# A graph network's last three edge passes: TensorE's gather of a batch cut into parts between its other products

## The chip, the cores and the metric

One core of a Trainium2 chip runs the kernel. TensorE multiplies matrices, VectorE (DVE) and ScalarE (ACT) do elementwise work, GpSimd (POOL) issues indirect DMAs, SyncE (SP) issues the other DMAs. The metric is the device time in microseconds of one launch, of which the median of three runs is given.

## The reference

Four graph networks run one after the other on 6250 nodes with 16 features and 206,250 edges sorted by target node, each followed by a residual sum and a layer norm. The kernel numbers its edge passes 0 to 9: pass 0 is the first network, passes 1 to 6 the second, pass 7 the third, passes 8 and 9 the two rounds of the fourth. The last two networks are those that the change touches:

```
# third: pass 7
msg = inputs[src] * timestamp
h = jax.ops.segment_max(msg, dst, num_segments=inputs.shape[0])
x = layernorm(x + h @ W.T + b)

# fourth: its first layer is computed in pass 7, the rounds are passes 8 and 9
w = relu(edgefeats @ fnet_w1 + fnet_b1) @ fnet_w2 + fnet_b2
W = w.reshape(-1, 16, 16)
for _ in range(2):
    xj = hx[edge_src]
    m = einsum('ei,eio->eo', xj, W)
    agg = segment_sum(m, edge_dst, num_segments=n_nodes) * inv_deg
    hx = gru_cell(agg, hx, ...)
```

## The kernel before

**Batches.** The edges lie in tiles of 128. A batch has `HT` = 8 tiles, 1024 edges, and there are `NB` = 202 batches in each of passes 7, 8 and 9. The engines run their own instruction streams, in the order in which the code issues them, and wait on semaphores. The order is written out by hand; for these three passes there is no planner. Each engine does one loop body a batch: `maxima(k)` in pass 7, `messages8(k)` (ScalarE: `next_hot(k)`) in passes 8 and 9.

**Where the source features come from.** Each tile needs the 16 features of its 128 source nodes. Five of the eight tiles of a batch (`FETCHED`) get them by an indirect DMA of GpSimd (L781). The other three (`GT`, 384 edges) get them from TensorE, in four steps. VectorE makes one-hot rows of the source's block with seven `tensor_scalar` operations (`hot_rows`, L1635; two buffers `hot8`). TensorE multiplies them with the node table `x8`, which is cut into three bf16 pieces: 6 blocks x 3 pieces = 18 products of 384 columns (L835) and a last one with 96 rows (L836), all added up in one PSUM bank, `picked_rows` (`gather8`). VectorE keeps of each sum the row of the right node (`select8`, L1644) and writes it to SBUF (`picked_by`, two buffers). TensorE turns the result with three fp32 products, which the profile shows as six (`turn8`, L845), and ScalarE copies it from PSUM (`copy8`, L1464).

**The order and its waits.** There is one bank `picked_rows`. `gather8(p, j)` waits until the one-hot rows of batch j are made (`hot8_made`) and until batch j - 1 was selected (`selected`), and signals `picked` with its last product. `select8(p, j)` waits for `picked` of j, `turn8(p, j)` for `selected` of j and the copy of j - 1. All this runs ahead of the batch that uses it: in the body of batch k, TensorE turns batch k + 3 (`AHEAD` = 3) and gathers batch k + 4; VectorE makes the one-hot rows of k + 5 and selects k + 4. The first four gathers come before the loop (`open_gather`).

**TensorE's other work in a batch.** Segment products (`segments`, L824): eight fp32 products, shown as 16, which add the values of batch k - 1 into two open PSUM banks by target node. They wait for the masked values of VectorE (`split_blocks`, L1538) and the one-hot of ScalarE (`one_hot`, L1435). In pass 7: a transpose into the scan (L1122), one out of it (L1138), and the first layer of the fourth network, four row-tiled products (L1130, shown as eight), after which ScalarE applies the relu (L1485) and stores the result. In passes 8 and 9: the messages, bias products (L1170) and second-layer products (L1174), into four banks, in two halves, each with a signal; VectorE multiplies them with the source features in four operations (L2197) and adds up (L2204).

TensorE's order in a batch before the change is, in pass 7: transpose in, turn of k + 3, first layer, gather of k + 4, segment products of k - 1, transpose out. In passes 8 and 9: messages of k, turn of k + 3, gather of k + 4, segment products of k - 1.

VectorE's order is, in pass 7: values of k - 1, two steps of the reset, weighted message of k + 1, scan (L2164), carry, one-hot rows of k + 5, select of k + 4. In passes 8 and 9: four multiplications, one-hot rows of k + 5, reduction, select of k + 4, values of k. ScalarE's is, in pass 7: copy of k + 3, relu of the first layer, eight squares (L1429), store, one-hot; in passes 8 and 9: squares, copy of k + 3, one-hot.

Of the kernel before, what the change touches and what calls it, by code (L numbers as in the profile page):

```python
# [47 lines left out]
NB = -(-TE // (2 * HT)) * 2  # L48
# [16 lines left out]
GC = GT * P  # L65
FETCHED = HT - GT
AHEAD = 3
STRIPS = 4
SE = HE // STRIPS
BL = 7  # L70
BLANES = P
LAST = BL - 1
# [35 lines left out]
def build(nc, a, out):  # L108
# [12 lines left out]
    with ctx:  # L121
# [688 lines left out]
        def _(pe):  # L810
# [5 lines left out]
            def segments(p, k, h):  # L816

                pe.load(out_at, base[0:1, ds(k * HT + HT, HT)])
                outs = [pe.snap(r, min_val=0, max_val=2 * CH - 32) for r in out_at]
                pe.wait_ge(scl[p].sem, scl[p].at(k - 1, APER[p]))  # L820
                pe.wait_ge(vec[p].sem, vec[p].at(k + 1, VALUES7) if p == 7 else vec[p].at(k, VALUES8))
                pe.sem_inc(pe_go, 1)
                for u in range(HT):
                    last = mm(sums[:, ds(outs[u], 32)], hot[h][:, u, :], masked[h][:, u, :, :].rearrange("p b f -> p (b f)"),  # L824
                              start=False, stop=False)
                last.then_inc(ten[p].sem, 1)

            def gather8(p, j):

                pe.wait_ge(hot8_made[p], j + 1)  # L830
                pe.wait_ge(selected[p], j)
                pe.sem_inc(pe_go, 1)
                for b in range(LAST):
                    for i in range(3):
                        mm(picked_rows, x8[:, b, i, :], hot8[j % 2][:, b, :], start=b == i == 0, stop=False)  # L835
                last = mm(picked_rows, x8[0:STACKED, LAST, 0, :], hot8[j % 2][0:STACKED, LAST, :],  # L836
                          start=False, stop=True)
                last.then_inc(picked[p], 1)

            def turn8(p, j):  # L840

                pe.wait_ge(selected[p], j + 1)
                pe.wait_ge(copied[p], j)
                for u in range(GT):
                    last = mm(turned_rows[:, u * 16:(u + 1) * 16], picked_by[j % 2][:, u * P:(u + 1) * P], pick_f,  # L845
                              start=True, stop=True)
                last.then_inc(turned[p], 1)
# [263 lines left out]
            p = 7  # L1111
# [5 lines left out]
            def maxima(k):  # L1117
                h = k % 2

                pe.wait_ge(vec[p].sem, vec[p].at(k - 1, VPER[p] if k == 0 else MSG))  # L1120
                pe.wait_ge(vec[p].sem, vec[p].at(k - 1, SCAN))
                nc.tensor.transpose(ps[:, 4, 0:P], msg[h][:, :, :].rearrange("p u f -> p (u f)"), w["ident"][:, :]  # L1122
                                    ).then_inc(ten[p].sem, 1)
                if k + AHEAD < NB:
                    turn8(p, k + AHEAD)
                pe.wait_ge(loaded[h], load_count(p, k))
                pe.wait_ge(scl[p].sem, scl[p].at(k - 1, RELU7))
                pe.sem_inc(pe_go, 1)
                for i in range(STRIPS):
                    last = mm(ps[32 * i:32 * i + 32, 7, 0:SE], w["f1"][32 * i:32 * i + 13, :], edges[h][32 * i:32 * i + 13, :],  # L1130
                              start=True, stop=True)
                last.then_inc(ten[p].sem, 1)
                if k + AHEAD + 1 < NB:
                    gather8(p, k + AHEAD + 1)
                segments(p, k - 1, 1 - h)
                pe.wait_ge(vec[p].sem, vec[p].at(k, SCAN))
                pe.sem_inc(pe_go, 1)
                nc.tensor.transpose(ps[:, 6, 0:P], wk[:, HE:HE + P], w["ident"][:, :]).then_inc(ten[p].sem, 1)  # L1138
# [16 lines left out]
            for p in (8, 9):  # L1155
                pe.wait_ge(ready, SETUP + 3 + 2 * (p - 7))
                pe.wait_ge(bias_cut, BIAS_CUT)
                stage_done(pe, PHASES[p])
                open_sums()
                ten[p].open(pe)  # L1160
                open_gather(p)
                def messages8(k):
                    h = k % 2

                    pe.wait_ge(loaded[h], load_count(p, k))
                    for strips, used in ((range(2), MUL[1]), (range(2, STRIPS), MUL[3])):
                        pe.wait_ge(vec[p].sem, vec[p].at(k - 1, used))
                        pe.sem_inc(pe_go, 1)
                        for i in strips:
                            mm(ps[:, 4 + i, :], ones16[32 * i:32 * i + 32, :],  # L1170
                               bias3[32 * i:32 * i + 32, :].unsqueeze(1).to_broadcast([32, 2, 256]), start=True, stop=False)
                        for v in range(2):
                            for i in strips:
                                last = mm(ps[:, 4 + i, v * 256:(v + 1) * 256], strip[h][32 * i:32 * i + 32, v * P:(v + 1) * P],  # L1174
                                          w["w2b"][32 * i:32 * i + 32, :], start=False, stop=v == 1)
                        last.then_inc(ten[p].sem, 1)

                    if k + AHEAD < NB:
                        turn8(p, k + AHEAD)
                    if k + AHEAD + 1 < NB:  # L1180
                        gather8(p, k + AHEAD + 1)
                    segments(p, k - 1, 1 - h)

                for k in range(NB):
                    messages8(k)
                segments(p, NB - 1, 1)
                close_sums()
                turn_sums(p)
                name = PHASES[p + 1]
                for c in range(2):  # L1190
                    pe.wait_ge(*after(name, c, 2))
                    for g in range(2):
                        mm(bank(c, g), ih_pk[g], t_pk[:, pcs(c)], start=True, stop=False)
                        mm(bank(c, g), hh_pk[g], hidden(p)[:, pcs(c)], start=False, stop=True)
                    mm(bank(c, 3), ih_pk[2], t_pk[:, pcs(c)], start=True, stop=True)
                    mm(bank(c, 2), hh_pk[2], hidden(p)[:, pcs(c)], start=True, stop=True).then_inc(packed[name][c], 1)
                if p == 8:
                    packed_rows(name, 10, h_pk)
                else:
                    packed_norm(name, 11)  # L1200
                    packed_rows(name, 18, x_pk)
# [3 lines left out]
        def _(act):  # L1205
# [273 lines left out]
            cut8(7)  # L1479
            def maxima(k):  # L1480
                h = k % 2
                if k + AHEAD < NB:
                    copy8(7, k + AHEAD)
                act.wait_ge(ten[7].sem, ten[7].at(k, F7))
                act_fn(rst, ps[:, 7, 0:SE], ACT.Relu, bias=w["fb1"][:, :]).then_inc(scl[7].sem, 1)  # L1485
                squares(7, k + 1, 1 - h, rel_last)
                act.wait_ge(scl[7].sem, scl[7].at(k, RELU7))
                act.dma_start(rT[:, ds(k * SE, SE)], rst).then_inc(r_out, 16)
                act.wait_ge(ten[7].sem, ten[7].at(k, SEG7))
                one_hot(7, k + 1, 1 - h)  # L1490
                act.wait_ge(r_out, k * 16 + 16)

            for k in range(NB):
# [6 lines left out]
            for p in (8, 9):  # L1500
                open_one_hots(p, rel)
                cut8(p)
                def next_hot(k):
                    h = k % 2
                    squares(p, k + 1, 1 - h, rel)
                    if k + AHEAD < NB:
                        copy8(p, k + AHEAD)
                    act.wait_ge(ten[p].sem, ten[p].at(k, SEG8))
                    one_hot(p, k + 1, 1 - h)

                for k in range(NB):
                    next_hot(k)
                join(p)
                name = PHASES[p + 1]
                for c in range(2):
                    act.wait_ge(*after(name, c, 3))
                    for g in range(2):
                        act_fn(gates[:, g, pcs(c)], bank(c, g), ACT.Sigmoid, bias=bias_pk[:, 4 + g:5 + g])
                    act_fn(gates[:, 2, pcs(c)], bank(c, 2), ACT.Identity, bias=bias_pk[:, 3:4]).then_inc(packed[name][c], 1)
                packed_one(name, 6, u_pk, t_pk, ACT.Tanh, bias=bias_pk[:, 2:3])  # L1520
                if p == 8:
                    packed_rows(name, 11, 3)
                else:
                    packed_norm(name, 11)
                    packed_rows(name, 19, 4)
# [765 lines left out]
```

## Time and profile before

| what | value |
|---|---|
| median of 3 runs | 8719.59 us (8715.59 to 8722.13) |
| profiled execution, first to last instruction | 10879.2 us |
| time of that execution apart from its span | not given |
| TensorE's mean granted clock | 0.867 of full speed |
| pass 7, scans from / to | 5140.4 / 6915.0 us |
| pass 8, reductions from / to | 7072.1 / 8879.9 us |
| pass 9, reductions from / to | 9036.9 / 10829.0 us |

The profile is of one execution, whose span is longer than the time of the runs without a profiler. Its times are in microseconds from its first instruction unless marked ns. PE is TensorE, PEld its weight loads. In a timeline each row is a group of like instructions: start, duration, engine, line, operation, what it writes and reads, and behind [ the idle time of the engine before it and what ended that. "issue" is a wait that nothing in the profile explains, "remote" one that was ended by a semaphore update whose maker the profile doesn't tell. In a row of windows stand the stretch, its length, the busy time of PE, PEld, DVE, ACT and POOL with the number of instructions, the granted clock of TensorE as a share of full speed, the DMA engines' busy share and GB/s. The ends of products are modelled.

### The profile page before, as it was taken

How to read it: one execution, taken by the hardware profiler on the slowest of the kernel's cores; microseconds unless marked ns; L12 is line 12 of the kernel's file. 1: busy time of each engine (PE TensorE's matmuls, PEld its weight loads, DVE VectorE, ACT ScalarE, POOL GpSimd, SP SyncE). 2: the span in 40 equal slices, each digit the busy share in tenths (PEclk: the TensorE clock that was granted, in tenths of full speed). 3: DMA queues.
4: the chain of work that ended last, by engine and by line, in shares of the span. 5: the costliest groups of instructions: out<-in, count | busy, mean ns of one | idle time of the engine just before them, and what ended most of it. 6: DMA issues, size and time to landing. Idle time of an engine off the chain costs nothing.

```text
span 10879.2 us, 202778 instructions
## 1 busy us (share of the span) xinstructions
PE 8956.7 (82%) x67778; PEld 6273.6 (58%) x67782; DVE 6315.3 (58%) x13443; ACT 3593.0 (33%) x10701; POOL 4698.0 (43%) x4703
## 2 busy tenths in 40 slices
PE   1588877888887999974888888599999977999998
PEld 0345544555555878862565556466666655666666
DVE  2577766777763222222444444377777766777877
ACT  5233322333330011000444444344443433444444
POOL 1456555666560000003555555355555535555552
PEclk9889988999996999975888888788888888888888
DMA  9522233222228978994222222111111111111111
GB/s 315 165 77 80 80 87 83 82 82 81 79 71 327 323 277 282 321 354 155 63 62 63 62 62 63 41 42 41 41 42 41 42 34 35 42 42 42 42 41 33
DMA packets 915020, 1169.57 MB, mean 108 GB/s; under 512 B 245746, under 2 KB 807652, under 8 KB 913804
## 3 DMA queue, kind: packets, MB, share of 16 engines
q1 hardware_dynamic: 720778, 1086.22, 30.9%
q0 software_dynamic: 150336, 28.94, 3.4%
q10 hardware_dynamic: 43202, 44.90, 1.3%
q8 instruction: 456, 7.47, 0.3%
q14 instruction: 248, 2.03, 0.1%
HBM read 1025.39 MB, written 133.22 MB: 106 GB/s over the span
## 4 chain that ended last, share of the span: by engine, by line
PE 50%; issue 6%; DVE 6%; another core or an unknown queue 5%; DMA 3%; ACT 1%; SPq 0%; DVEq 0%; ACTq 0%
PE ps L835 18%; PE ps L1036 9%; PE ps L824 8%; PE ps L845 4%; PE ps L1174 4%; DMA arena<-adj 3%; PE ps L1053 1%; PE ps L1170 1%; PE ps L1130 1%; DVE msg L2204 1%; PE ps L1047 1%; PE ps L836 1%; DVE dinv L1635 1%; DVE invdeg L1635 1%
## 5 line engine op out<-in xcount | busy, mean ns | idle before, releaser
L781 POOL DMA_INDIRECT arena<-tab,x_all x3030 | 2951.3, 974 | 4504.7 <-DMA tab<-stage 2048.9
L799 POOL DMA_INDIRECT adj<-acc x1616 | 1693.0, 1048 | 1266.4 <-DVE acc L1851 721.7
L835 PE MATMUL ps<-invdeg,acc 128*128 128x384 bf16 x5454 | 1202.4, 387 | 154.9 <-issue 154.5
L835 PE MATMUL ps<-dinv,acc 128*128 128x384 bf16 x5454 | 1221.2, 392 | 95.8 <-issue 49.2
L1246 ACT ACTIVATE wide<-ps,not_all 128x128 bf16<-128x128 f32 x1616 | 658.2, 419 | 1552.1 <-remote 1030.9
L1644 DVE SCALAR_TENSOR_TENSOR dinv<-x_all,ps 128x384 f32<-128x384 f16 x606 | 368.3, 608 | 1160.5 <-remote 825.0
L835 PEld LDWEIGHTS ps<-invdeg,acc 128*128 128x128 bf16 x5454 | 619.0, 118 | 697.2 <-issue 485.6
L835 PEld LDWEIGHTS ps<-dinv,acc 128*128 128x128 bf16 x5454 | 624.2, 119 | 651.6 <-issue 449.1
L1429 ACT ACTIVATE arena<-w_iota,rel 128x128 f32<-128x128 f32 x3232 | 988.2, 388 | 13.1
L845 PE MATMUL ps<-x_all,dinv 128*128 128x16 f32 x3636 | 585.9, 287 | 398.8 <-issue 290.8
L845 PEld LDWEIGHTS ps<-x_all,dinv 128*128 128x128 f32 x3636 | 537.7, 220 | 579.2 <-issue 450.6
L913 PE MATMUL ps<-arena 128*128 128x128 f32 x3232 | 481.9, 294 | 360.3 <-issue 180.5
L1435 ACT ACTIVATE acc<-arena,unit 128x1024 f32<-128x1024 f32 x303 | 348.0, 1149 | 1190.0 <-PE ps L824 433.1
L1435 ACT ACTIVATE arena<-arena,unit 128x1024 f32<-128x1024 f32 x303 | 348.1, 1149 | 1183.4 <-PE ps L824 451.8
L1806 DVE TENSOR_TENSOR arena<-ps,threes 128x1024 bf16<-128x1024 f32 x606 | 718.4, 1212 | 0.0
L913 PEld LDWEIGHTS ps<-arena 128*128 128x128 f32 x3232 | 439.8, 206 | 422.6 <-issue 301.1
L2197 DVE TENSOR_TENSOR arena<-ps,arena 128x512 f32<-128x512 f32 x808 | 504.7, 682 | 294.1 <-remote 163.9
L2197 DVE TENSOR_TENSOR dinv<-ps,arena 128x512 f32<-128x512 f32 x808 | 504.1, 682 | 288.2 <-remote 157.8
L824 PEld LDWEIGHTS ps<-acc 128*128 128x128 f32 x4896 | 615.0, 198 | 95.2 <-issue 76.8
L1036 PE MATMUL ps<-x_all,arena 128*128 128x192 bf16 (+1 forms) x8232 | 595.5, 234 | 89.7 <-DMA arena<-adj 89.5
L824 PE MATMUL ps<-acc 128*128 128x32 f32 x4896 | 605.1, 276 | 64.6 <-issue 62.5
L824 PEld LDWEIGHTS ps<-acc,arena 128*128 128x128 f32 x4848 | 602.2, 196 | 82.1 <-issue 64.3
(351 smaller groups left out, 14631.1 us busy)
## 6 DMA issues: line engine op xcount, KB each, us to landing
arena<-adj SPq DMA_DIRECT2D x588, 896.0 KB, 5.6
x_all<-src_parts SPq DMA_DIRECT2D x606, 192.0 KB
arena<-rels SPq DMA_DIRECT2D x202, 512.0 KB
arena<-tab SPq DMA_DIRECT2D x1616, 64.0 KB
adj<-zero SPq DMA_DIRECT2D x28, 3136.0 KB
arena<-rT SPq DMA_DIRECT2D x404, 128.0 KB
arena<-tab,x_all POOLq DMA_INDIRECT x3030
adj<-acc POOLq DMA_INDIRECT x1616
```

Source lines behind the costliest of these rows:

```text
L781: pool.indirect_dma_start(G[b][:, u, :], None, TABLE[PHASES[p]], bass.IndirectOffsetOnAxis(ap=idx[:, t:t + 1], axis=0)).then_inc(gathered[ ...
L799: pool.indirect_dma_start(adj_cells, bass.IndirectOffsetOnAxis(ap=pair[:, t, 0:1], axis=0), pair16[:, t, 2:3], None).then_inc(celled[g], 16)
L824: last = mm(sums[:, ds(outs[u], 32)], hot[h][:, u, :], masked[h][:, u, :, :].rearrange("p b f -> p (b f)"), start=False, stop=False)
L835: mm(picked_rows, x8[:, b, i, :], hot8[j % 2][:, b, :], start=b == i == 0, stop=False)
L845: last = mm(turned_rows[:, u * 16:(u + 1) * 16], picked_by[j % 2][:, u * P:(u + 1) * P], pick_f, start=True, stop=True)
L913: last = mm(ps[:, 2 + u // 4, (u % 4) * P:(u % 4 + 1) * P], hotT[h][:, u * P:(u + 1) * P], nodes0[h][:, u, :], start=True, stop=True)
L1036: last = mm(ps[:, 2 * par + u // 2, u % 2 * W:(u % 2 + 1) * W], ring[n % RING][:, s, u * P:(u + 1) * P], rows[:, j * SC + s, :, :].rearran ...
L1246: act_fn(junk[u % 2][:, 0:(u % R + 1) * P], equal_to(u), ACT.Relu, bias=not_all[:, :], accum_out=equals[h][:, u:u + 1]).then_inc(scl[0].se ...
L1429: last = act_fn(far2[:, u, :], w["iota"][:, :], ACT.Square, scale=-1.0, bias=r[:, tile(k, u):tile(k, u) + 1])
L1435: act_fn(hot[h][:, :, :], far2[:, :, :], ACT.Relu, scale=-2.0, bias=unit[:, :]).then_inc(scl[p].sem, 1)
L1806: tt(placed[h][:, i, :, :, :], hot_a[:, :, :].unsqueeze(3).to_broadcast([P, HT, A8, 16]), threes[h][:, :, i, :].unsqueeze(2).to_broadcast( ...
L2197: tt(products[h][:, q * 512:(q + 1) * 512].rearrange("p (u o i) -> p u o i", u=2, i=16), ps[:, 4 + q, :].rearrange("p (u o i) -> p u o i", ...
```

## The change

TensorE's `gather8` is cut into a first part (`gather8_open`, with the two waits), a middle one (`gather8_blocks`) and a last one (`gather8_close`, with the signal). The instructions are the same. Their order in a batch becomes, in pass 7: transpose in, 9 products of the gather of k + 4, first layer, segment products of k - 1, turn of k + 3, the other 10 products of the gather, transpose out. In passes 8 and 9: messages of k, 6 products of the gather of k + 4, segment products of k - 1, 6 products of the gather, turn of k + 3, the last 7 products of the gather. ScalarE's copy of k + 3 moves behind the one-hot. VectorE, GpSimd and SyncE keep their order.

```diff
+CUT8 = 2, 4
+HALF8 = 3
...
-            def gather8(p, j):
+            def gather8_open(p, j, upto):
                 pe.wait_ge(hot8_made[p], j + 1)
                 pe.wait_ge(selected[p], j)
                 pe.sem_inc(pe_go, 1)
-                for b in range(LAST):
+                gather8_blocks(j, 0, upto)
+
+            def gather8_blocks(j, lo, hi):
+                for b in range(lo, hi):
                     for i in range(3):
                         mm(picked_rows, x8[:, b, i, :], hot8[j % 2][:, b, :], start=b == i == 0, stop=False)
+
+            def gather8_close(p, j, at):
+                gather8_blocks(j, at, LAST)
                 last = mm(picked_rows, x8[0:STACKED, LAST, 0, :], hot8[j % 2][0:STACKED, LAST, :],
                           start=False, stop=True)
                 last.then_inc(picked[p], 1)
@@ TensorE, pass 7, maxima
-                if k + AHEAD < NB:
-                    turn8(p, k + AHEAD)
+                if k + AHEAD + 1 < NB:
+                    gather8_open(p, k + AHEAD + 1, HALF8)
...
                 last.then_inc(ten[p].sem, 1)
+                segments(p, k - 1, 1 - h)
+                if k + AHEAD < NB:
+                    turn8(p, k + AHEAD)
                 if k + AHEAD + 1 < NB:
-                    gather8(p, k + AHEAD + 1)
-                segments(p, k - 1, 1 - h)
+                    gather8_close(p, k + AHEAD + 1, HALF8)
@@ TensorE, passes 8 and 9, messages8
+                    gathering = k + AHEAD + 1 < NB
+                    if gathering:
+                        gather8_open(p, k + AHEAD + 1, CUT8[0])
+                    segments(p, k - 1, 1 - h)
+                    if gathering:
+                        gather8_blocks(k + AHEAD + 1, *CUT8)
                     if k + AHEAD < NB:
                         turn8(p, k + AHEAD)
-                    if k + AHEAD + 1 < NB:
-                        gather8(p, k + AHEAD + 1)
-                    segments(p, k - 1, 1 - h)
+                    if gathering:
+                        gather8_close(p, k + AHEAD + 1, CUT8[1])
@@ ScalarE, pass 7, maxima
-                if k + AHEAD < NB:
-                    copy8(7, k + AHEAD)
...
                 one_hot(7, k + 1, 1 - h)
+                if k + AHEAD < NB:
+                    copy8(7, k + AHEAD)
@@ ScalarE, passes 8 and 9, next_hot
                     squares(p, k + 1, 1 - h, rel)
+                    act.wait_ge(ten[p].sem, ten[p].at(k, SEG8))
+                    one_hot(p, k + 1, 1 - h)
                     if k + AHEAD < NB:
                         copy8(p, k + AHEAD)
-                    act.wait_ge(ten[p].sem, ten[p].at(k, SEG8))
-                    one_hot(p, k + 1, 1 - h)
```

## Rows read from the trace of the kernel before

**Rows 1.** Page, busy us by engine (share of the span) and instructions.
```profile
PE 8956.7 (82%) x67778; PEld 6273.6 (58%) x67782; DVE 6315.3 (58%) x13443; ACT 3593.0 (33%) x10701; POOL 4698.0 (43%) x4703
```

**Rows 2.** Windows of passes 7, 8, 9; behind the engines: clock, DMA share, GB/s.
```profile
5150.00:6850.00 1700.00, 1486.21 (x9688) 1011.11 (x9688) 728.90 (x2661) 770.58 (x2090) 885.57 (x922) 0.83 0.26 63
7050.00:8850.00 1800.00, 1642.21 (x12024) 1170.04 (x12025) 1408.07 (x2761) 737.30 (x1971) 916.35 (x934) 0.87 0.19 41
9040.00:10840.00 1800.00, 1639.36 (x12172) 1179.27 (x12174) 1429.45 (x2781) 753.52 (x2009) 910.13 (x927) 0.88 0.19 41
```

**Rows 3.** Source views, scan and reduction of a batch: durations, first and last start.
```profile
L2164 DVE TENSOR_TENSOR_SCAN arena<-arena,carry,ps x202: 467/473/481, 5140.4 to 6915.0; 128x128 f32<-128x128 f32 x101
...
L2204 DVE TENSOR_REDUCE msg<-arena x101: 2270/2276/2287, 7072.1 to 8873.6; 128x128 f32<-128x2048 f32 x101
L2204 DVE TENSOR_REDUCE msg<-dinv x101: 2271/2275/2286, 7082.2 to 8879.9; 128x128 f32<-128x2048 f32 x101
```

**Rows 4.** Timeline, pass 8, TensorE: start, us, what [idle before <-releaser].
```profile
8065.56 0.39 PE L1170 MATMUL ps<-x_all,ones 32*128 32x512 bf16 x2
...
8066.98 0.84 PE L845 MATMUL ps<-x_all,dinv 128*128 128x16 f32 x6
8067.68 3.09 PE L835 MATMUL ps<-invdeg,acc 128*128 128x384 bf16 x18
8070.60 0.33 PE L836 MATMUL ps<-invdeg,acc 96*128 96x384 bf16 x1
8070.77 1.87 PE L824 MATMUL ps<-acc,arena 128*128 128x32 f32 x16
8072.56 0.39 PE L1170 MATMUL ps<-x_all,ones 32*128 32x512 bf16 x2
...
8073.01 1.05 PE L1174 MATMUL ps<-w_w2b,arena 32*128 32x256 f32 x14
```

**Rows 5.** Timeline, pass 8, the batches after, VectorE and TensorE.
```profile
8077.04 2.48 DVE L2197 TENSOR_TENSOR arena<-ps,arena 128x512 f32<-128x512 f32 x4 [2.94 <-remote]
...
8083.24 0.60 DVE L1644 SCALAR_TENSOR_TENSOR dinv<-x_all,ps 128x384 f32<-128x384 f16 x1
...
8083.90 1.46 PE L845 MATMUL ps<-x_all,dinv 128*128 128x16 f32 x6 [2.44 <-issue]
8084.10 2.48 DVE L2197 TENSOR_TENSOR dinv<-ps,arena 128x512 f32<-128x512 f32 x4
...
8085.20 5.75 PE L835 MATMUL ps<-invdeg,acc 128*128 128x384 bf16 x18
```

**Rows 6.** Windows, pass 8: behind the gap.
```profile
8083.90:8090.90 7.00, 7.00 (x25) 4.06 (x26) 6.47 (x13) 0.21 (x1) 4.95 (x5) 0.52 0.29 55
```

**Rows 7.** Timeline, pass 7, TensorE.
```profile
6043.02 1.87 PE L824 MATMUL ps<-acc,arena 128*128 128x32 f32 x16
6044.73 0.31 PE L1138 MATMUL ps<-w_ident,arena 128*128 128x128 f32 x1
...
6044.98 0.74 PE L845 MATMUL ps<-x_all,dinv 128*128 128x16 f32 x6
...
6046.31 4.64 PE L835 MATMUL ps<-dinv,acc 128*128 128x384 bf16 x18
6050.79 0.33 PE L836 MATMUL ps<-dinv,acc 96*128 96x384 bf16 x1
```

**Rows 8.** Windows, pass 7: unbroken stretch without gather, and what follows.
```profile
6043.00:6046.30 3.30, 3.30 (x34) 2.77 (x32) 1.81 (x6) 1.25 (x2) 0.00 (x0) 0.96 0.23 50
6046.30:6047.30 1.00, 1.00 (x8) 0.49 (x5) 0.97 (x5) 0.88 (x3) 0.88 (x1) 0.50 0.19 55
```

**Rows 9.** Timeline, pass 7, VectorE's select.
```profile
6051.15 0.61 DVE L1644 SCALAR_TENSOR_TENSOR dinv<-x_all,ps 128x384 f32<-128x384 f16 x1 [2.80 <-PE ps L836]
```

**Rows 10.** Lines, pass 7: busy us, mean ns, idle us before and releasers.
```profile
L781 POOL DMA_INDIRECT arena<-tab,x_all x890 | 855.2, 961 | 744.5 <-DVE msg L2139 516.7 <-issue 226.6 <-DVE arena L2154 1.2
...
L1644 DVE SCALAR_TENSOR_TENSOR dinv<-x_all,ps 128x384 f32<-128x384 f16 x177 | 108.2, 611 | 651.4 <-remote 431.8 <-PE ps L836 193.8 <-issue 25.8
```

More of the change, by code:

```diff
@@ L838, in gather8 @@
                 last.then_inc(picked[p], 1)
+            def gather8(p, j):
+                gather8_open(p, j, CUT8[0])
+                gather8_close(p, j, CUT8[0])
             def turn8(p, j):
```

## The prediction, made before the change was run

> **What bounds the kernel now.** I read the page first: TensorE is busy 82% of the span, VectorE and GpSimd under 60% [rows 1]. The change touches only the loops of passes 7, 8 and 9, so I cut the span at them: in all three TensorE is busy 87 to 91%, and its granted clock is 0.83 to 0.88 [rows 2]. First and last starts of one instruction a batch give the periods: pass 7 (6915.0 - 5140.4) / 201 = 8.83 us, pass 8 (8879.9 - 7072.1) / 201 = 8.99 [rows 3]; pass 9, with the same busy time in as long a stretch [rows 2], is taken like pass 8.
>
> The timeline shows what a batch costs when nothing is late. In pass 8 the messages' first product starts at 8065.56 and again at 8072.56: 7.00 us of TensorE without a gap [rows 4]. It is made of messages 1.42 (8065.56 to 8066.98), turn 0.70, gather 2.92 + 0.17, segment products 1.79. VectorE needs as much: its products start at 8077.04 and, after an unbroken row of work, again at 8084.10, 7.06 us later [rows 5]. So in passes 8 and 9 the two engines are level, and VectorE's 7.06 is a floor that no order on TensorE lowers. What lifts the mean to 9 is seen at 8077.04: VectorE had waited 2.94 us for a release, although the product that gives it shows an end at 8073.01 + 1.05; then TensorE, having run ahead, waits 2.44 us for the select, its clock is 0.52 of full speed, near the lower of its two levels (1.2 of 2.4 GHz), in the 7 us that follow, and 18 products of the next gather take 5.75 us, not 3.09 [rows 4, 5, 6].
>
> In pass 7 VectorE is light. TensorE's batch is: segment products, two transposes, turn and first layer, 6043.02 to 6046.31 = 3.29 us, then the gather, 3.09 at full clock [rows 7, 4]: 6.38 us. Here too the clock falls, even with no gap: TensorE is busy 3.30 of the 3.30 us from 6043.00, and from 6046.3 the clock is 0.50 [rows 8].
>
> **The profile against the runs.** The traced span is 10,879.2 us (the page gives no other time for that execution), the median of the runs 8719.6, a fifth less. If the late releases belong to the traced execution alone, passes 8 and 9 run at their floor, 404 x 7.06 = 2852 us for 404 x 8.99 = 3632 traced, and pass 7 at 202 x 6.38 = 1289 for 1784. That is 1275 of the 2160 us between the two times, and the rest must come from the stages before 5140, which are more than half of the span of passes that don't change. I take this as the likeliest state of an unprofiled run: the batches near 7.0 and 6.4, not 9. The sum below is so made with durations of single instructions, which the traced span has in common with it, and what it gives is added to the median; on the trace's own time the pass 7 term would be the same or larger.
>
> **The change part by part.** No instruction of work is added or taken away; per pass 198 batches (202 less the four opened ahead) have a gather that is split.
>
> *Passes 8 and 9.* After the messages TensorE waited for the select of batch k+3 at the turn; it now waits for the same select at the first part of the gather. But the gather that this select reads now ends just before the messages, not before the segment products. From the gather's last product to the end of the select it is 0.33 + 0.03 + 0.61 = 0.97 us, and 0.06 more until TensorE starts [rows 4, 9, 5]. TensorE has 0.17 + 1.42 = 1.59 us of its own until then, so 0.56 us are left: no stall, but before they were 2.35. What this select needs of VectorE otherwise is not changed. The segment products now start behind six products (0.97 us); they need the masked values, which VectorE makes right behind the select, before its next products at 8084.10 [rows 5]. Queued behind the new wait are the segment products; ScalarE waits for these with its one-hot. Its work is 737 / 1800 of 8.99 = 3.7 us of a batch of 7 [rows 2], and the copy moved behind the one-hot is needed three batches later: hidden by these 3 us of idle time. With that cover gone the one-hot, and so the segment products, would be late by what ScalarE is over 7, nothing by these rows. Cutting the gather adds two changes a batch between bf16 and fp32 products. From the gather's last product to the segment products the step is 0.17 us, no more than between two gather products (2.92 / 18 = 0.162) [rows 4]. So value 0. At worst each new change costs one such step again, 0.34 a batch, of which 0.06 hides under VectorE: 0.28 x 396 = +111 us; at best the bf16 messages follow the bf16 gather better than they followed the segment products, 0.06 of TensorE's 7.00, which VectorE hides. A gain must come from the clock. At most it is all that lies over the floor, (8.99 - 7.06) x 404 = 780 us; but the clock falls there behind the 2.44 us gap [rows 5, 6], and the gap comes of the late release, which the order doesn't touch. Behind the clean batch from 8065.56 the gather runs at full speed in the old order. So value 0 for the clock, with up to -180 kept for the range.
>
> *Pass 7.* Here the same turn-about has no cover. The last part of the gather of batch k+3 is followed only by two transposes (6044.73 to 6044.98, 0.25 us) and then by the first part of the next gather, which may not write the bank before the select has read it. Ready at 0.17 + 0.25 = 0.42 us after the last product's start, TensorE is released at 1.03: a wait of 0.61 us in every batch, where before the segment products (1.71) lay over the select [rows 7, 4, 9]. VectorE itself is idle before that select (2.80 us [rows 9]), so it starts at once. Behind the waiting gather stand the first layer, the segment products and the turn, and by them ScalarE's relu and one-hot; all slip by the same 0.61 and no further, as ScalarE's work (771 / 1700 of 8.83 = 4.0 us a batch [rows 2]) is shorter than the batch. 198 x 0.61 = +121 us. Bounds: 0, if something else sets the pass at 7.0 (GpSimd's row gathers are five a batch, each 0.96 us and 226.6 / 890 = 0.25 of issue before it, 6.1 together [rows 10], so not by these rows), and +220 if the release comes half a microsecond later, as many do in the trace.
>
> The split gives back some clock in pass 7. The gather behind an unbroken stretch of 3.29 us took 6046.31 to 6050.79 = 4.48 us to its last product where 2.92 are clean: 1.56 lost [rows 7]. After the change the longest stretch without gather is 3.04 us (the transposes are out of it). I take one batch in five as falling before, and half of these still: 0.1 x 1.56 x 198 = -31. Ends: 0, and -150 if every second batch fell and none does now. Sum of the pass: +90. Of the stall nothing is made good later, since the next batch's select waits for the next gather.
>
> A rule to weigh: the Trainium skill, page "TensorE: Matmul & The Clock Gate", section "Why this matters for your kernels", has the clock drop after a pause of TensorE between bursts of products. The fall behind a gap agrees with it [rows 5, 6]; the one behind a full stretch does not [rows 8], and there the row decides. By the page's rule alone the split in pass 7 would earn nothing.
>
> Sum: 8719.6 + 121 - 31 = about 8810 us.
>
> **Rivals.**
> *The clock pays (faster).* If unprofiled runs also have gaps and falls, say a mean of 7.5 us in passes 8 and 9, spreading the gather holds the clock and returns 0.45 x 404 = -180; with pass 7's +90 it is 8630. For it: clocks of 0.87 and 0.88 in the trace; against it: those falls follow gaps, and VectorE's floor. It decides if the mean batch is over 7.3. Chance 0.22.
> *No earnings of the clock in pass 7.* +121 alone, 8841: one rule for the clock in both orders, gaps alone matter. For it the fall behind the gap [rows 6]; against it the one without [rows 8]. Chance 0.08.
> *Pass 7 is hurt more.* Its gather now waits for the select, which waited 432 us for unexplained releases in the trace [rows 10]; and at half clock the halves of the gather are short, so that the clock may come back later. Another 0.5 us a batch: 8900. Chance 0.08.
> *Nothing.* The stall is hidden since the pass is set by what no row shows, or stall and clock cancel: 8720. Chance 0.12.
> *Forecast*, 8770 to 8850: chance 0.50.
>
> **How the numbers follow.** Slower by over 0.2% (17 us, about what this measurement can tell from no change): 0.50 + 0.08 + 0.08 = 0.66. Within: 0.12. Faster: 0.22. The range 8640 to 8900 takes in all but half of the fast case and part of the worst one. The forecast's own range is 8770 to 8850.
>
> **What would show it.** In pass 7's timeline a gap of about 0.6 us on TensorE before the first part of the gather, released by the select, in nearly every batch, and a longer period; in passes 8 and 9 clean batches of 7.06 us as before and no gap before the first part. In the traced execution, whose releases are late, the gaps of pass 7 would be wider. I am wrong if passes 8 and 9 show clearly fewer falls of the clock and the runs are faster; or if pass 7 has the gap and no longer period.

## The result, and the profile after

| | median | runs |
|---|---|---|
| before | 8720.86 us | 4 (8715.59 to 8727.43) |
| after | 8815.02 us | 4 (8808.77 to 8816.81) |

The ratio is 1.0107, with a 95% interval of 1.0095 to 1.0120: slower by 94 us, where +90 was forecast. The kernel before, unchanged, took 8713 to 8721 us in some sessions on a chip and 10,911 to 10,922 in others, and the trace shown ahead (10,879.2) is of the second sort, while that of after (8814.7 us of span, 8816.52 for the execution) is of the first; so every experiment below stands beside the kernel before of its own session.

The page of after: busy time, then TensorE's granted clock in 40 slices (slices 20 to 27 hold pass 7):

```profile
PE 7994.8 (91%) x67778; PEld 5757.5 (65%) x67782; DVE 6250.7 (71%) x13443; ACT 3566.7 (40%) x10701; POOL 4802.5 (54%) x4703
...
PEclk9999999999986999997799999989999998999998
```

Windows of passes 7 and 8, as in [rows 2]; then, as in [rows 3], scan of pass 7 and reductions of pass 8 with first and last start:

```profile
4340.00:5780.00 1440.00, 1341.03 (x10048) 919.80 (x10046) 748.70 (x2750) 799.61 (x2170) 931.71 (x975) 0.97 0.32 77
5870.00:7270.00 1400.00, 1397.08 (x12057) 1023.58 (x12059) 1398.05 (x2754) 730.86 (x1981) 1040.38 (x978) 1.00 0.25 53
```
```profile
L2186 DVE TENSOR_TENSOR_SCAN arena<-arena,carry,ps x202: 467/474/480, 4328.3 to 5789.6; 128x128 f32<-128x128 f32 x101
...
L2226 DVE TENSOR_REDUCE msg<-arena x101: 2266/2268/2286, 5863.5 to 7274.2; 128x128 f32<-128x2048 f32 x101
L2226 DVE TENSOR_REDUCE msg<-dinv x101: 2266/2267/2286, 5870.5 to 7280.5; 128x128 f32<-128x2048 f32 x101
```

In pass 8 both engines are busy for all of the time, VectorE 1398.05 of 1400 us, and the batch takes (7280.5 - 5863.5) / 201 = 7.05 us: the floor of [rows 5]. Pass 9 is alike, at 7.04. In pass 7 TensorE is busy 93%, and the batch takes (5789.6 - 4328.3) / 201 = 7.27 us. Its timeline, TensorE and then VectorE's select, shows where from:

```profile
4779.82 0.33 PE L846 MATMUL ps<-invdeg,acc 96*128 96x384 bf16 x1
4779.98 0.27 PE L1155 MATMUL ps<-w_ident,arena 128*128 128x128 f32 x1
4780.10 0.27 PE L1137 MATMUL ps<-w_ident,msg 128*128 128x128 f32 x1
4780.90 1.62 PE L841 MATMUL ps<-dinv,acc 128*128 128x384 bf16 x9 [0.53 <-issue]
4782.45 0.63 PE L1145 MATMUL ps<-arena,w_f 13*32 13x256 f32 x8
4783.02 1.97 PE L826 MATMUL ps<-acc 128*128 128x32 f32 x16
...
4786.95 0.33 PE L846 MATMUL ps<-dinv,acc 96*128 96x384 bf16 x1
```
```profile
4780.18 0.61 DVE L1666 SCALAR_TENSOR_TENSOR dinv<-x_all,ps 128x384 f32<-128x384 f16 x1 [3.21 <-PE ps L846]
```

The gather's last product starts at 4779.82, the select 0.36 later, and the next gather's first part 1.08 after that last product. The next batch repeats it: 4786.95 - 4779.82 = 7.13 us. Waits of pass 7 from 4400 to 5750 us, 1350 / 7.27 = 186 batches (total us, times, longest):

```profile
DVE dinv L1666 <- PE ps L846: 619.6, 181, 4.4
...
PE ps L841 <- issue: 93.1, 185, 0.5
```

TensorE waits in all but one batch, 0.5 us counted from the modelled end of the second transpose, and never longer. The view can't name the releaser, but the select's end, 4780.18 + 0.61 = 4780.79, is 0.11 us before the product.

### The profile page after: what moved, and what is told of

Same layout as the page of the kernel before. It is cut to its first block, busy times and chain, and to the rows that moved or that the text cites. A ratio compares the mean times of both kernels' runs of the same rounds, so it can differ in the third digit from the quotient of the medians.

```text
span 8814.7 us, 202778 instructions
## 1 busy us (share of the span) xinstructions
PE 7994.8 (91%) x67778; PEld 5757.5 (65%) x67782; DVE 6250.7 (71%) x13443; ACT 3566.7 (40%) x10701; POOL 4802.5 (54%) x4703
## 4 chain that ended last, share of the span: by engine, by line
PE 86%; SPq 5%; DMA 4%; issue 2%; DVE 2%; ACT 0%; DVEq 0%; ACTq 0%; PEldq 0%
PE ps L841 21%; PE ps L981 18%; PE ps L826 13%; PE ps L1051 11%; PE ps L1191 5%; PE ps L860 4%; PE ps L928 4%; DMA arena<-adj 3%; SPq L678 3%; PE ps L1187 2%; PE ps L1068 2%; PE ps L1145 1%; PE ps L846 1%; PE ps L936 1%; PE ps L1062 1%
## 5 line engine op out<-in xcount | busy, mean ns | idle before, releaser
L783 POOL DMA_INDIRECT arena<-tab,x_all x3030 | 3112.1, 1027 | 3039.5 <-DMA tab<-stage 2006.2
L841 PE MATMUL ps<-dinv,acc 128*128 128x384 bf16 x5454 | 1038.5, 331 | 97.2 <-issue 50.8
L841 PE MATMUL ps<-invdeg,acc 128*128 128x384 bf16 x5454 | 1032.2, 329 | 52.7 <-issue 52.5
L841 PEld LDWEIGHTS ps<-dinv,acc 128*128 128x128 bf16 x5454 | 520.3, 106 | 450.3 <-issue 204.6
L841 PEld LDWEIGHTS ps<-invdeg,acc 128*128 128x128 bf16 x5454 | 518.3, 105 | 401.1 <-issue 153.4
L1051 PEld LDWEIGHTS ps<-x_all,arena 128*128 128x128 bf16 x8232 | 556.7, 103 | 156.3 <-DMA arena<-adj 103.7
L1051 PE MATMUL ps<-arena 128*128 128x192 bf16 (+1 forms) x8232 | 603.8, 237 | 50.0 <-DMA arena<-adj 49.9
L1051 PEld LDWEIGHTS ps<-arena 128*128 128x128 bf16 x8232 | 571.6, 105 | 116.8 <-DMA arena<-adj 56.4
L826 PE MATMUL ps<-acc,arena 128*128 128x32 f32 x4848 | 603.8, 279 | 3.6 <-issue 3.0
L1657 DVE TENSOR_SCALAR dinv<-x_all 128x384 bf16<-128x384 f16 x2121 | 521.3, 312 | 18.0 <-DMA x_all<-src_parts 17.9
```

The lines of the kernel that those rows point to most:

```text
L783: pool.indirect_dma_start(G[b][:, u, :], None, TABLE[PHASES[p]], bass.IndirectOffsetOnAxis(ap=idx[:, t:t + 1], axis=0)).then_inc(gathered[ ...
L1051: last = mm(ps[:, 2 * par + u // 2, u % 2 * W:(u % 2 + 1) * W], ring[n % RING][:, s, u * P:(u + 1) * P], rows[:, j * SC + s, :, :].rearran ...
L1657: last = ts(hot8[j % 2][:, b, :], parts_row[j % SL][0:BLANES, 0:GC], lane_b[0:BLANES, b:b + 1], None, ALU.is_equal)
```

## The experiments

**Session 1: which part costs.** The kernel before takes 10,910.67 us here.

`e0_before_again` is the kernel before, unchanged.

> The unchanged kernel before, traced once more: the first trace of it was 2160 us longer than its runs, while the trace of the changed kernel was as long as its runs. Theory A (late releases belong to that one traced execution): the span is about 8720, passes 8 and 9 run at 7.05 us a batch, pass 7 at the changed kernel's 7.27 less 94/202 = 6.8. If the clock falls without any gap, pass 7's 6.8 is 6.4 of work and 0.4 for falls, with a granted clock under 0.95. Theory B (the kernel before really runs at 8.8 to 9 us a batch in these passes): the span is about 10,880 again, and the time between the kernels went elsewhere.

10,900.69 us, span 10,898.9, clock 0.866. The scans of pass 7 run from 5158.1 to 6933.2: 8.83 us a batch as in [rows 3], and the runs without a profiler take as long. That is the second of the two theories: the late releases come with the session, not with one traced execution.

`e1_only_8_9` is after with the old pass 7:

```
 in maxima(k), and ScalarE's copy of pass 7 back in its place:
-                if k + AHEAD + 1 < NB:
-                    gather8_open(p, k + AHEAD + 1, HALF8)
+                if k + AHEAD < NB:
+                    turn8(p, k + AHEAD)
                 ... first layer
+                if k + AHEAD + 1 < NB:
+                    gather8(p, k + AHEAD + 1)
                 segments(p, k - 1, 1 - h)
-                if k + AHEAD < NB:
-                    turn8(p, k + AHEAD)
-                if k + AHEAD + 1 < NB:
-                    gather8_close(p, k + AHEAD + 1, HALF8)
```

> Passes 8 and 9 in the new order, with ScalarE's copy behind the one-hot; pass 7 as before. My theory: no change, ratio 1.000 within 0.001 (8721), both at VectorE's floor of 7.05 us a batch. Rival (the cut gather costs TensorE two changes of type a batch, or the smaller slack before the select bites): up to +111 us, 1.013. Rival (the clock pays in these passes): under 0.998, and then pass 7 alone has lost more than the whole difference.

11,135.39 us, ratio 1.0215 (1.0187 to 1.0243), where 1.000 was expected. Reductions of pass 8:

```profile
L2224 DVE TENSOR_REDUCE msg<-arena x101: 2274/2281/2287, 7129.2 to 9036.2; 128x128 f32<-128x2048 f32 x101
L2224 DVE TENSOR_REDUCE msg<-dinv x101: 2275/2280/2286, 7138.1 to 9042.6; 128x128 f32<-128x2048 f32 x101
```

That is (9042.6 - 7129.2) / 201 = 9.52 us, against 8.97 in `e0_before_again`: where releases come late, the new order of passes 8 and 9 costs 0.55 us a batch in pass 8 and 0.67 in pass 9 (9.62 for 8.95), and the medians differ by 225 us. Its timeline, VectorE and then TensorE:

```profile
8026.34 2.28 DVE L2224 TENSOR_REDUCE msg<-arena 128x128 f32<-128x2048 f32 x1
8028.53 0.61 DVE L1664 SCALAR_TENSOR_TENSOR dinv<-x_all,ps 128x384 f32<-128x384 f16 x1
```
```profile
8025.95 0.33 PE L846 MATMUL ps<-dinv,acc 96*128 96x384 bf16 x1
...
8026.65 1.05 PE L1189 MATMUL ps<-w_w2b,arena 32*128 32x256 f32 x14
8029.25 1.14 PE L841 MATMUL ps<-invdeg,acc 128*128 128x384 bf16 x6 [1.55 <-issue]
8030.49 3.36 PE L826 MATMUL ps<-acc,arena 128*128 128x32 f32 x16
```

VectorE, itself behind, selects at 8028.53; TensorE has nothing else and waits 1.55 us for it, and the segment products behind that gap take 3.36 us, not 1.87. The granted clock is 1.00 up to 8030.50, the gap included, and 0.54 from there to 8034.00: it fell behind the gap.

`e2_only_7` is the other half: after with the old order of passes 8 and 9.

```
 in messages8(k), and ScalarE's copy of passes 8 and 9 back in its place:
-                    if gathering:
-                        gather8_open(p, k + AHEAD + 1, CUT8[0])
-                    segments(p, k - 1, 1 - h)
-                    if gathering:
-                        gather8_blocks(k + AHEAD + 1, *CUT8)
                     if k + AHEAD < NB:
                         turn8(p, k + AHEAD)
-                    if gathering:
-                        gather8_close(p, k + AHEAD + 1, CUT8[1])
+                    if k + AHEAD + 1 < NB:
+                        gather8(p, k + AHEAD + 1)
+                    segments(p, k - 1, 1 - h)
```

> Pass 7 in the new order, with its copy behind the one-hot; passes 8 and 9 as before. My theory: the whole loss is here, +94 us, ratio 1.0108 (8815). Rival (it is in passes 8 and 9): 1.000.

11,090.56 us, 1.0174 (1.0137 to 1.0211). The scans run from 5175.6 to 7130.4: 9.73 us a batch, 0.90 more than in `e0_before_again`. Passes 8 and 9 are at 8.93 and 8.94. So the whole difference of this kernel, 180 us, lies in pass 7, but here it is twice the 94 us expected.

`e3_two_banks` takes the cause of pass 7's wait away. It is after, but in pass 7 the gathers of odd batches go to another PSUM bank, so that a gather needs the select of two batches ago only.

```
+        def picked_bank(p, j):
+            return ps[:, 5, 0:GC] if p == 7 and j % 2 else picked_rows
                 ... in gather8_open; products and select use picked_bank(p, j)
                 pe.wait_ge(hot8_made[p], j + 1)
-                pe.wait_ge(selected[p], j)
+                pe.wait_ge(selected[p], j - 1 if p == 7 and j else j)
```

> The changed kernel, but in pass 7 the gathers of odd batches write PSUM bank 5, which is free there, so that the first part of a gather waits for the select of two batches earlier. Nothing else is changed. My theory (the stall before the first part of the gather, 0.50 us a batch in the changed kernel's trace, is the loss): the stall goes, pass 7's batch is 7.27 - 0.50 = 6.8 us or less, the kernel is at 8720 or below, ratio to before 0.990 to 1.001; if the clock then also keeps up, the floor is 6.4 us a batch and 8635, ratio 0.990. Rival (the loss is the clock, or the many small parts themselves, not the wait): the ratio stays at 1.008 to 1.011 without a gap before the gather.

11,132.53 us, 1.0205 (1.0174 to 1.0236). Scans from 5173.4 to 6935.3: pass 7 is back at 8.77 us, a little under the 8.83 of before; 9.53 and 9.60 in passes 8 and 9 keep the rest, so that the ratio stays above the 0.990 to 1.001 expected.

**Session 2: the same again.** The kernel before takes 10,921.7 us here, so `f0_before_third`, `f1_only_8_9` and `f3_two_banks` are repeats of `e0_before_again`, `e1_only_8_9` and `e3_two_banks`.

> The unchanged kernel before, traced once more beside the next three. The last four kernels ran on a chip on which the kernel before takes 10,910 us in every run, not 8720, and showed signals of TensorE up to 3 us late; the changed kernel's trace, from the chip of 8815 us, has none of these. So the two traces first compared are of two chips. Theory A (the chip decides, not the kernel): on a chip that gives 8720 this trace has no late signal, passes 8 and 9 at 7.05 us a batch, pass 7 at about 6.8 us with a clock that falls now and then behind a stretch without gather; on the other chip it is as the traces of 10,880 and 10,899 us.

10,918.38 us; 8.84, 8.97 and 8.96 us a batch in passes 7, 8 and 9.

> Passes 8 and 9 alone in the new order, once more. It was 1.0215 on the chip of 10,910 us, with batches of 9.5 and 9.6 us where the kernel before has 8.97 and 8.95: there TensorE's signals come late and the slack before the select is 0.56 us, not 2.35. My theory for a chip without late signals: 7.05 us a batch in both orders, ratio 1.000 within 0.001. If it is again a chip of 10,910: 1.021 again. Rival (the parts themselves cost): over 1.002 on the chip of 8720 as well.

11,171.29 us, 1.0224 (1.0205 to 1.0242); 8.91, 9.54, 9.58.

> The changed kernel with two banks for pass 7's gathers, once more. On the chip of 10,910 its pass 7 took 8.77 us a batch against 9.73 with one bank in the same order, and 8.83 in the kernel before. My theory for a chip without late signals: pass 7 loses the 0.50 us wait and most falls of the clock and goes to 6.4 to 6.8 us, ratio 0.990 to 1.001 to before; the changed kernel is at 1.0107. Rival (the wait is not the loss): 1.008 to 1.011.

11,168.91 us, 1.0228 (1.0210 to 1.0247); pass 7 at 8.90. All three as in session 1.

`f4_segments_last` is a version built from before. It cuts the gather in pass 7 for the clock, but keeps the segment products between a gather's end and the next one's start; passes 8 and 9 and ScalarE are as before.

```
                 in maxima(k): transpose in
                 if k + AHEAD < NB:
                     turn8(p, k + AHEAD)
+                if k + AHEAD + 1 < NB:
+                    gather8_open(p, k + AHEAD + 1, HALF8)
                 ... first layer
                 if k + AHEAD + 1 < NB:
-                    gather8(p, k + AHEAD + 1)
+                    gather8_close(p, k + AHEAD + 1, HALF8)
                 segments(p, k - 1, 1 - h)
                 ... transpose out
```

> The kernel before, with pass 7's gather cut in two around the first layer alone: turn, 9 products of the gather, first layer, the other 10, then the segment products, as before, so that they cover the select. Passes 8 and 9 and ScalarE as before. My theory: no wait for the select, and no stretch without gather longer than segment products, transposes and turn, 2.6 us for 3.3, so that the clock does not fall: pass 7 at 6.4 us a batch for 6.8, 80 us less, ratio 0.991 (8640) on a chip without late signals. Rival (the cut itself costs, or the clock falls for another reason than the order): 0.998 to 1.003. On the chip of 10,910 us the clock falls behind waits for late signals, and I expect 0.99 to 1.00.

10,916.22 us, 0.9995 (0.9985 to 1.0005): no change; 8.91, 8.97, 8.94 us a batch. With late releases this cut earns nothing, and costs next to nothing (8.91 for 8.84 us in pass 7).

**Session 3, the kernel before at 8713.25 us: what sets the time of the result.**

`g5_slack_kept` is before, with the gather of passes 8 and 9 cut around the turn alone. The cut is there, the segment products still end the batch.

```
+                    if gathering:
+                        gather8_open(p, k + AHEAD + 1, CUT8[0])
                     if k + AHEAD < NB:
                         turn8(p, k + AHEAD)
-                    if k + AHEAD + 1 < NB:
-                        gather8(p, k + AHEAD + 1)
+                    if gathering:
+                        gather8_close(p, k + AHEAD + 1, CUT8[0])
                     segments(p, k - 1, 1 - h)
```

> Pass 7 as before. Passes 8 and 9: the gather is cut too, with its first 6 products ahead of the turn and right behind the messages, as in the changed kernel, but its last 13 products stand before the segment products, as before, so that these and the messages still cover the select (slack 2.35 us, not 0.56). On the chips of 10,910 us the changed order of passes 8 and 9 cost 0.55 to 0.6 us a batch, ratio 1.022. My theory (late signals eat the smaller slack): here the ratio is 0.998 to 1.003. Rival (cutting the gather, with its changes of type, costs where signals are late): 1.01 or more. On a chip of 8720 us both expect 1.000, passes 8 and 9 at 7.05 and pass 7, in its old order, at 6.8.

8719.96 us, 1.0007 (0.9997 to 1.0017). Passes 8 and 9 take 7.06 and 7.07 us. As its pass 7 is that of before, this trace also shows what the old order does at 8720 us. Scans and window of pass 7:

```profile
L2182 DVE TENSOR_TENSOR_SCAN arena<-arena,carry,ps x202: 465/473/481, 4322.3 to 5686.6; 128x128 f32<-128x128 f32 x101
```
```profile
4340.00:5680.00 1340.00, 1340.00 (x10007) 955.85 (x10007) 773.60 (x2735) 798.33 (x2166) 926.26 (x970) 0.92 0.35 82
```

(5686.6 - 4322.3) / 201 = 6.79 us with TensorE busy all the time, and yet a clock of 0.92. The timeline and the windows of two batches, a clean one and one in which it falls:

```profile
4730.22 3.10 PE L841 MATMUL ps<-dinv,acc 128*128 128x384 bf16 x18
4733.15 0.33 PE L846 MATMUL ps<-dinv,acc 96*128 96x384 bf16 x1
4733.32 1.87 PE L826 MATMUL ps<-acc 128*128 128x32 f32 x16
4735.02 0.31 PE L1153 MATMUL ps<-w_ident,arena 128*128 128x128 f32 x1
...
4735.95 0.63 PE L1145 MATMUL ps<-arena,w_f 13*32 13x256 f32 x8
4736.51 4.78 PE L841 MATMUL ps<-invdeg,acc 128*128 128x384 bf16 x18
4741.13 0.33 PE L846 MATMUL ps<-invdeg,acc 96*128 96x384 bf16 x1
```
```profile
4733.30:4736.50 3.20, 3.20 (x34) 2.77 (x32) 1.71 (x6) 1.25 (x2) 2.59 (x3) 1.00 0.40 102
4736.50:4740.20 3.70, 3.70 (x17) 1.79 (x14) 2.45 (x10) 2.80 (x9) 2.79 (x4) 0.54 0.28 69
```

From last product to last product it is 7.98 us here; counted over the pass, clean batches take 6.30 and 62 of 201 are long, at 7.95 each, nearly every third. In each the granted clock falls once, about the end of the stretch without gather.

`g4_segments_last` is the kernel of `f4_segments_last` again.

> Pass 7 cut around the first layer alone with the segment products last, once more: 0.9995 on a chip of 10,920 us, where pass 7 took 8.9 us a batch in this and in the old order. On a chip of 8720 us my theory expects pass 7 at 6.4 us for 6.8, ratio 0.991; the rival 0.998 to 1.003. On a chip of 10,920 us: 0.9995 again.

**8611.72 us, 0.9885 (0.9869 to 0.9902)**: it beats both kernels. Scans and window of pass 7, and its timeline:

```profile
L2181 DVE TENSOR_TENSOR_SCAN arena<-arena,carry,ps x202: 468/473/482, 4318.1 to 5579.4; 128x128 f32<-128x128 f32 x101
```
```profile
4340.00:5570.00 1230.00, 1229.97 (x9961) 885.85 (x9958) 778.61 (x2721) 792.71 (x2153) 923.31 (x966) 1.00 0.39 89
```
```profile
4733.84 1.62 PE L841 MATMUL ps<-dinv,acc 128*128 128x384 bf16 x9
4735.39 0.63 PE L1147 MATMUL ps<-arena,w_f 13*32 13x256 f32 x8
4735.96 1.64 PE L841 MATMUL ps<-dinv,acc 128*128 128x384 bf16 x9
4737.43 0.33 PE L846 MATMUL ps<-dinv,acc 96*128 96x384 bf16 x1
4737.60 1.87 PE L826 MATMUL ps<-acc 128*128 128x32 f32 x16
...
4739.56 0.74 PE L860 MATMUL ps<-x_all,dinv 128*128 128x16 f32 x6
4740.15 1.62 PE L841 MATMUL ps<-invdeg,acc 128*128 128x384 bf16 x9
```

(5579.4 - 4318.1) / 201 = 6.28 us at a clock of 1.00, and no batch is long. From the last product to the next gather 2.72 us pass, all of them work, so the select (ready after 1.08) is never waited for. The gain in pass 7 is (6.79 - 6.28) x 201 = 103 us; the medians differ by 101.5.

`g3_two_banks` is the kernel of `e3_two_banks` again.

> The changed kernel with two banks for pass 7's gathers, once more: 1.0205 and 1.0228 on two chips of 10,910 us, of which 1.022 is the new order of passes 8 and 9. On a chip of 8720 us my theory expects the changed kernel's 1.0107 to fall to 1.001 or below (6.4 to 6.8 us a batch for 7.27); the rival (the wait is not the loss) 1.008 to 1.011.

8720.95 us, 1.0007 (0.9998 to 1.0017). That is 94 us under after's median, and 86 if each is set against the kernel before of its own session; pass 7 takes (5693.2 - 4326.8) / 201 = 6.80 us a batch for 7.27, 94 us in all. Its timeline, TensorE in pass 7, and the pass's window:

```profile
4735.41 0.33 PE L850 MATMUL ps<-invdeg,acc 96*128 96x384 bf16 x1
...
4735.79 1.62 PE L845 MATMUL ps<-dinv,acc 128*128 128x384 bf16 x9
4737.35 0.63 PE L1149 MATMUL ps<-arena,w_f 13*32 13x256 f32 x8
4737.91 1.97 PE L830 MATMUL ps<-acc 128*128 128x32 f32 x16
4739.72 0.82 PE L864 MATMUL ps<-x_all,dinv 128*128 128x16 f32 x6
4740.39 1.62 PE L845 MATMUL ps<-dinv,acc 128*128 128x384 bf16 x9
4741.85 0.33 PE L850 MATMUL ps<-dinv,acc 96*128 96x384 bf16 x1
```
```profile
4340.00:5680.00 1340.00, 1339.56 (x10016) 941.16 (x10014) 758.56 (x2743) 795.87 (x2162) 932.97 (x974) 0.94 0.34 82
```

Without the wait the next gather starts 0.38 us after the last product, and a clean batch takes 6.44 us. The clock still falls, in 46 batches. That it equals the kernel before is chance: 0.14 us more in a clean batch, fewer falls.

The rows tell where the 0.14 us come from. The 18 wide gather products take 3.02 us in two parts (4735.79 to 4737.35, 4740.39 to 4741.85) and 2.93 in one (4730.22 to 4733.15 in `g5_slack_kept`); the segment products take 1.81 us to the turn behind them (4737.91 to 4739.72) and 1.70 to a transpose (4733.32 to 4735.02).

**Session 4, before at 8719.51 us: what holds passes 8 and 9.** `h6_less_vector` is `g4_segments_last`, but in passes 8 and 9 it leaves out one of VectorE's seven one-hot operations of a batch, that of block 5, so that source features from this block are not those of the reference.

```
-                for b in range(BL):
+                for b in range(BL) if p == 7 else (0, 1, 2, 3, 4, 6):
```

> The kernel with the segment products last (0.9885 where the kernel before takes 8713 us), and in passes 8 and 9 VectorE leaves out one of the seven one-hot operations of a batch (the rows of block 5 stay those of an earlier pass), 0.24 us less of its 7.05. Theory A (VectorE sets these passes and TensorE, with 7.00 a batch, stands right behind it): the batch falls from 7.05 to 6.95 to 7.00, 20 to 40 us, ratio 0.984 to 0.986 at 8713 us. Theory B (TensorE has room to spare): it falls by all of 0.24, 97 us, ratio 0.977. Theory C (VectorE is not the bound): 7.05 stays, 0.9885. At 10,910 us, where late signals set the batch, all three expect 0.99 to 1.00.

8585.65 us, 0.9848 (0.9830 to 0.9865). Pass 8:

```profile
L2221 DVE TENSOR_REDUCE msg<-arena x101: 2269/2274/2286, 5656.6 to 7053.0; 128x128 f32<-128x2048 f32 x101
L2221 DVE TENSOR_REDUCE msg<-dinv x101: 2265/2274/2286, 5663.4 to 7059.2; 128x128 f32<-128x2048 f32 x101
```

(7059.2 - 5656.6) / 201 = 6.98 us, from 7.04. VectorE's 7.05 was the bound; freed of 0.24 us of one-hot work it gives 0.07 us, and then TensorE's 7.0 holds: from 5700 to 7050 us TensorE is busy 1348.59 of the 1350 us, VectorE 1336.14.

## Why the prediction was right, step by step

The forecast of 8810 us (8770 to 8850) stands against 8815. The old order's pass 7 is taken from `g5_slack_kept` (6.787 us a batch), since no trace of the kernel before itself is of the 8720 us sort. Against it the sum comes out so; each number is one per batch times 201:

| step | predicted | measured |
|---|---|---|
| passes 8 and 9, cut, waits and copy | 0 | 0: 7.04 to 7.07 us a batch in before's order (`g4_segments_last`), cut (`g5_slack_kept`) and after |
| pass 7, wait for the select | +121 (0.61 us) | +139 (7.13 - 6.44 = 0.69 us) |
| pass 7, the cut order in itself | 0 | +28 (6.44 - 6.30 = 0.14 us) |
| pass 7, clock given back | -31 | -70 (98 us of falls in the old order, 28 in the new) |
| sum | +90 | +97; pass 7's traces 7.27 - 6.787 = 0.48 us, 97; medians 94 |

- *The wait* is shown: it stands in after's timeline in 185 of 186 batches; a second bank removes it, and 86 to 94 us with it (`g3_two_banks`). The release was predicted at 1.03 us after the last product's start, and came at 1.08; TensorE was to be ready at 0.42, and was at 0.38. VectorE had been idle for some 3 us before the select (619.6 us in 181 waits), so nothing on its side made it late.
- *The clock* was mis-sized on both sides. I took one batch in five as falling, and half of these as saved. It was nearly one in three (62 of 201, 1.65 us each, near the 1.56 of [rows 7]). That half are saved was about right: in after's pass 7 the granted clock falls 29 times. But each fall costs less there, 28 / 29 = 0.97 us. It is mostly spread over two batches, and the low stretch takes in the wait; how much of the difference that makes wasn't measured. The count can't be read in a trace with late releases, where gaps and falls mix.
- *The cut order in itself* was costed at nothing in pass 7, although the same step, 0.17 us between gather and fp32 products, was weighed as a bound for passes 8 and 9. A clean batch got 0.14 us longer: some 0.1 by the cut of the wide products, 0.1 by segment products with the turn behind them, less some hundredths elsewhere (the rows of `g3_two_banks`). In `g4_segments_last` the cut costs the same (1.55 + 1.47 us), but the segment products keep their transposes, and the turn with gather products behind it takes 4739.56 to 4740.15 = 0.59 us for 0.67: the clean batch stays at 6.3. Why a product is slower behind one kind than behind another is not shown.
- *The two errors*, +46 (wait and cut order) and -39 (clock), cancel by luck. The mechanism and the sign of each term were right but for the cut order; that the sum is off by only 7 us is no measure of how well its terms were known.
- *Passes 8 and 9 at their floor* is shown by 1.00 of clock, by VectorE busy 1398.05 of 1400 us and by `h6_less_vector`. The rival in which the clock pays needed a mean batch over 7.3 there, and the mean was 7.05.
- *"If the late releases belong to the traced execution alone"* was right in what it was used for and wrong in its words. The traces of runs near 8720 us show batches at the floor, but in the long sessions every run is long, profiled or not. Of the 2160 us, 885 were put before pass 7, and most of them are found there: the scans of pass 7 start at 5158.1 us in `e0_before_again` and at 4322.3 in `g5_slack_kept`.
- *The clean batch of pass 7* was read 0.08 us too long, 6.38 for 6.30: the stretch of 3.29 us in [rows 7] ends in a first layer of 0.66 us (6045.65 to 6046.31), which takes 0.57 where the clock is full (4735.95 to 4736.51). The sum doesn't use it.
- *The weighed rule.* By the Trainium skill, "TensorE: Matmul & The Clock Gate", section "Why this matters for your kernels", the clock drops after a pause. The fall behind the 1.55 us gap of `e1_only_8_9` is of this kind, though the page speaks of longer pauses. The 98 us that pass 7 loses to the clock in the old order are of another: it falls with TensorE busy 3.20 of 3.20 us, and a kernel that changes only the order of busy work takes all of it away.

What stays open: whether cut or lost slack (0.56 us for 2.35) costs the 0.55 us a batch in the long sessions, as `g5_slack_kept` wasn't run in one; the timeline of `e1_only_8_9` speaks for the slack, and so does `f4_segments_last`, whose cut in pass 7 left the cover in place and cost under 0.1 us a batch. Open is also why the clock falls 29 times in after and 47 in `g3_two_banks`, with the same 3.04 us between the parts of the gather.

## What to carry to other kernels

When a product stream is reordered around a single buffer, measure what lies between the last write, the reader and the next write: the work put there must last longer than the round trip (1.08 us here), or the stall comes back in every batch. Cutting a long gather to spread it is worth as much as the clock it keeps, and only if that cover is left: a gather cut in two in pass 7 gave -101 us with the segment products over the round trip (`g4_segments_last`) and +94 without (after). A second buffer in place of the cover only brought the time back to that of the kernel before (`g3_two_banks`): its order costs 0.14 us more in a clean batch and keeps 47 falls. Look for falls of the clock in stretches without any gap as well.

## What the runs showed of the hardware that was not expected

- The granted clock fell from 1.00 to 0.54, that is from 2.4 to near 1.2 GHz, behind 3.20 us in which TensorE was busy without a gap, but with segment products, transposes, turn and first layer alone. Longest such stretch and falls in pass 7: 3.20 us and 63 (`g5_slack_kept`), 3.04 us and 29 (after) or 47 (`g3_two_banks`), 2.55 us and none (`g4_segments_last`, 4737.60 to 4740.15).
- One kernel takes 8713 to 8721 us or 10,911 to 10,922. Pass 7 takes 8.83 us a batch for 6.79, pass 8 8.97 for 7.05, and some 840 us of the difference lie before pass 7. Whether it is the chip or a state of it the runs don't tell; sessions 2 and 3, one of each sort, carry the same chip number.
- A handover from TensorE to VectorE and back costs little: 0.36 us from the start of the last product (0.33 us long) to the select, 0.11 from the select's end to the next product.
